# Moving one batch of the shared experts beside the row scatter, and splitting the filling products behind the routed experts

## The chip, the cores and the metric

The kernel runs on one core of one Trainium2 chip. The time is device microseconds (us) for one execution of the whole program, and the number to compare is the median over several executions. The core has five engines that run at the same time and wait for each other by semaphores: TensorE (PE, matrix products; PEld is its weight load), VectorE (DVE), ScalarE (ACT), GpSimd (POOL) and SyncE (SP, which issues DMAs here).

## The reference

Two decoder layers over x of 4 batches x 512 tokens x 128 features. Each layer adds self-attention, cross-attention to 77 context rows, and a mixture of experts, each on a layer-normalised x. The change is in the mixture of layer 0:

```python
logits = flat @ gate_w                                   # 2048 tokens, 16 experts
scores = softmax(logits) + gate_b
_, topi = top_k(scores, 2)
# each expert: its 320 best tokens of those that chose it (capacity)
idx = top_k(where(assigned, w_tok, -inf), capacity)
y = (silu(xs @ w1) * (xs @ w3) @ w2) * w_tok             # routed, on gathered rows xs
out = zeros.at[idxs].add(ys)
shared = mean over 2 shared experts of (silu(flat @ sw1) * (flat @ sw3)) @ sw2
x = x + out + shared                                     # then layer 1: attention of layernorm(x)
```

## The kernel before

The order on each engine is written out by hand; nothing reorders it but the waits. PSUM has eight banks of 128 x 512 floats, called bank[0] to bank[7]. X holds the residual x; a "batch" is 512 tokens, B = 4, QT = 4 tiles of 128 tokens in each.

**Layer 0's experts.** After the router, DVE works out, for each token and each of its two choices, the row of its expert's list (g_row). Then POOL writes the normalised tokens into the lists in DRAM by 32 indirect DMAs (L658, tensor xs_rows, 2 choices x 16 tiles). SP loads the lists back when all have landed (L510). The routed experts then run on PE, ACT, DVE and POOL in four turns of four experts (routed_turn, the last three in a loop), and SP stores the results (ys_rows, L514). When all are stored, POOL gathers the two result rows of each token of batch 0 by eight indirect DMAs (L670, into big_q and big_k; semaphore got[0]); the gathers of the other batches are spread over layer 1's attention.

**The shared experts** need no list, only hT, the transposed normalised tokens, so they fit anywhere. A unit u = 0 to 15 is a quarter of a batch's hidden features (c = u // 4 is the batch): PE forms two 128 x 512 products in shared_up (L1452; each f32 product shows as two passes in the trace), in banks 4 to 7; ACT takes silu of one (L969), DVE multiplies both (shared_hid, L2223). When the four units of a batch are there, shared_down (L1462, 16 products of 128 x 128, 32 passes) forms the batch's output in bank 0 or 7, and DVE adds half of it to X (shared_add, L2228, semaphore sh_x). Before, batches 0 and 1 (units 0 to 7, then down 0 and down 1) run beside the scatter, and batches 2 and 3 behind the routed experts, both in the order of all units first, then both downs.

**Filling products.** keep_busy (L1182) multiplies an identity into an unused bank; the result is never read. There are three in front of the routed experts (they wait for r_pad, which POOL sets by a memset between its last two scatters, L657), four behind the shared experts, and seven before the first scores of the attention.

**The start of layer 1's attention.** DVE's pre_norm(0, ...) adds the gathered rows of batch 0, weighted, to X (add_expert, L2255, four calls that each raise f0_x by one, so f0_x is 4 when the batch is complete), takes statistics (L1824, L1866), a scale by a few tiny steps, and writes ln_h (L2265, semaphore la_h). PE transposes ln_h (L1552), ACT copies it (L1023), and the projections, the spreading of queries and keys by DMA, and then the scores (L1633) follow. DVE's shared_add of the last two batches stands behind ln_h.

Of the kernel before, what the change touches and what calls it, by code (L numbers as in the profile page):

```python
# [14 lines left out]
ALU = mybir.AluOpType  # L15
# [4 lines left out]
P = 128  # L20
B, SEQ, D = 4, 512, 128
# [9 lines left out]
NSH = 2  # L31
# [73 lines left out]
def decoder_kernel(nc, a, out):  # L105
    ctx = ExitStack()
    with ctx:
# [10 lines left out]
        def sem(name):  # L118
            return ctx.enter_context(nc.semaphore(name))

        psum = ctx.enter_context(nc.psum_tensor("psum", [P, 8, 512], F32))
        bank = [psum[:, i, :] for i in range(8)]
# [112 lines left out]
        sh_hidden = [arena[:, 1 + i, :, :] for i in range(2)]  # L235
# [111 lines left out]
        sh_h, sh_silu, sh_hid, sh_y, sh_x, f0_x = (  # L347
            sem(n) for n in ("sh_h", "sh_silu", "sh_hid", "sh_y", "sh_x", "f0_x"))
# [70 lines left out]
        def f1_of(it, p):  # L419

            return {(11, 0): (0, 0), (11, 3): (0, 1), (12, 0): (1, 0), (12, 3): (1, 1), (15, 3): (2, 0), (15, 4): (2, 1)}.get((it, p))

        PRE_NORM = {1: 1, 3: 2, 7: 3}
        ADD_AT = {(1, False): 1, (2, True): 2, (6, True): 3}
        X1_NORM = {b * QT: b - 1 for b in range(1, B)}
        F1_NORM = {(10, False): 0, (11, True): 1, (14, True): 2}
        SCALE_AT = {(it, 5): ("pre", b) for it, b in PRE_NORM.items()}
        SCALE_AT.update({(it, 7): ("x1", b) for it, b in X1_NORM.items()})
        SCALE_AT.update({(9, 7): ("f1", 0), (11, 2): ("f1", 1), (14, 6): ("f1", 2)})

        def scale_count(kind, b):

            return NT + B + [SCALE_AT[at] for at in sorted(SCALE_AT)].index((kind, b))
# [160 lines left out]
        def _(pool):  # L594
# [32 lines left out]
            def batch_norm(b, scales, h):  # L627
                bt = slice(b * QT, (b + 1) * QT)
                pool.wait_ge(ln_mean_ok, scales)
                for _ in range(3):  # L630
                    chained(pool.tensor_tensor(ln_new[:, bt], ln_rstd[:, bt], ln_var[:, bt], ALU.mult))
                    chained(pool.tensor_tensor(ln_new[:, bt], ln_new[:, bt], ln_rstd[:, bt], ALU.mult))
                    chained(pool.tensor_scalar(ln_new[:, bt], ln_new[:, bt], -0.5, 1.5, ALU.mult, ALU.add))
                    chained(pool.tensor_tensor(ln_rstd[:, bt], ln_rstd[:, bt], ln_new[:, bt], ALU.mult))
                chained(pool.tensor_tensor(ln_h[:, bt, :], X[:, bt, :], bcast(ln_mv[:, bt, 0], 2, D), ALU.subtract))
                pool.tensor_tensor(ln_h[:, bt, :], ln_h[:, bt, :], bcast(ln_rstd[:, bt], 2, D), ALU.mult).then_inc(h, 1)
# [107 lines left out]
            def add_experts(b):  # L744
                pool.wait_ge(got[b], 16 * 2 * QT)
                for c in range(2):
                    if c:
                        pool.wait_ge(f0_x, b * 4 + 2)
                    bt = slice(b * QT, (b + 1) * QT)
                    chained(pool.tensor_tensor(gathered[c][:, bt, :], gathered[c][:, bt, :], bcast(g_w[:, c, bt], 2, D), ALU.mult))  # L750
                    pool.tensor_tensor(X[:, bt, :], X[:, bt, :], gathered[c][:, bt, :], ALU.add).then_inc(f0_x, 2)

            def guest_norm(it, late):
                if (it, late) in ADD_AT:
                    add_experts(ADD_AT[it, late])
                if late and it in PRE_NORM:
                    b = PRE_NORM[it]
                    batch_norm(b, scale_count("pre", b), la_h)
# [71 lines left out]
        def _(act):  # L830
# [134 lines left out]
            def shared_silu(u):  # L965
                act.wait_ge(sh_h, u + 1)
                if u >= 2:
                    act.wait_ge(sh_hid, u - 1)
                act.activation(silu[:, u % 2, :], bank[4 + 2 * (u % 2)][:, :], ACT.Silu).then_inc(sh_silu, 1)  # L969
# [11 lines left out]
            def routed_turn(j, first):  # L981
                for k in range(4):
                    routed_silu(j * 4 + k)
                    if k:
                        routed_y(j, k - 1)
                    if k in (0, 2) and not first:
                        act.wait_ge(ys_out[k // 2], j * 16)
                routed_y(j, 3)
# [16 lines left out]
            act.activation(k1T[:, :], bank[4][:, 0:B * LK], ACT.Identity, bias=x1b[:, 1:2]).then_inc(pre_act, 1)  # L1005
            act.wait_ge(pre_mm, 5)
            act.activation(vx1[:, :, :], bank[5][0:LK, :].rearrange("p (b d) -> p b d", b=B), ACT.Copy).then_inc(pre_act, 1)
            for u in range(8):
                shared_silu(u)
            routed_turn(0, True)  # L1010
            with act.Fori(1, E0 // 4) as j:
                routed_turn(j, False)
            for u in range(8, 16):
                shared_silu(u)
            warm(ACT.Exp)

# [158 lines left out]
        def _(pe):  # L1175
            def keep_busy(o, times, small=False):

                for _ in range(times):
                    if small:
                        pe.matmul(o[:, 0:P], ones[:, :], ones[:, :], start=True, stop=True)  # L1180
                    else:
                        pe.matmul(o, ident, cst[:, 0:SEQ], start=True, stop=True)  # L1182
# [154 lines left out]
            for b in range(B):  # L1337
                pe.wait_ge(ln_out, X0 * B + b + 1)
                for i in range(2):
                    mm = pe.matmul(bank[2 * b + i][:, :], x0w[:, i, :], hT[:, b * SEQ:(b + 1) * SEQ], start=True, stop=True)  # L1340
# [76 lines left out]
            for t in range(1, NT + 4):  # L1417
# [5 lines left out]
                u = (t - 3) // 2  # L1423
# [23 lines left out]
            def shared_up(u):  # L1447
                c, e = u // 4, E0 + u // 2 % 2
                if u >= 2:
                    pe.wait_ge(sh_hid, u - 1)  # L1450
                for w in range(2):
                    mm = pe.matmul(bank[4 + 2 * (u % 2) + w][:, :], w13[:, e, w, u % 2 * P:(u % 2 + 1) * P],  # L1452
                                   hT[:, c * SEQ:(c + 1) * SEQ], start=True, stop=True)
                mm.then_inc(sh_h, 1)

            def shared_down(c):
                pe.wait_ge(sh_hid, 4 * c + 4)
                if c >= 2:
                    pe.wait_ge(sh_x, c - 1)
                for t in range(QT):  # L1460
                    for k in range(4):
                        mm = pe.matmul(bank[7 * (c % 2)][:, t * P:(t + 1) * P], sh_hidden[c % 2][:, k, t * P:(t + 1) * P],  # L1462
                                       w2[:, E0 + k // 2, k % 2, :], start=(k == 0), stop=(k == 3))
                mm.then_inc(sh_y, 1)

# [45 lines left out]
            for i in range(2):  # L1511
                mm = pe.transpose(bank[1][:, i * P:(i + 1) * P], g_wm[:, i * NT // 2:(i + 1) * NT // 2, :].rearrange("p t e -> p (t e)"), ident)
# [8 lines left out]
            for i in range(2):  # L1521
                mm = pe.transpose(bank[1][:, i * P:(i + 1) * P], (g_lo, g_hi)[i][:, :].broadcast_to([P, P]), ident)
# [4 lines left out]
            pe.matmul(bank[3][:, :], ones[:, :], kinds, start=True, stop=True).then_inc(g_mm, 1)  # L1527
            pe.matmul(bank[2][:, :], tri, kinds, start=True, stop=True).then_inc(g_mm, 1)

            def shared_chunks(first, last):  # L1530
                for u in range(4 * first, 4 * last):
                    shared_up(u)
                for c in range(first, last):
                    shared_down(c)

            pe.wait_ge(pre_act, 3)
            shared_chunks(0, 2)
            pe.wait_ge(r_pad, 1)
            keep_busy(bank[2], 3)
            routed_turn(0, True)  # L1540
# [1 line left out]
                routed_turn(j, False)  # L1542
            routed_down(E0 - 1, 3, False)
            pe.wait_ge(r_yc, E0)
            shared_chunks(2, 4)
            pe.wait_ge(ld_a1, 112)
            def pre_part(b, part):
                o = pre_bank(b, part)
# [48 lines left out]
            def f1_part(b, part):  # L1597
# [6 lines left out]
                if part == 1:  # L1604
# [2 lines left out]
                        mm = pe.matmul(o[:, t * E1:(t + 1) * E1], hT_b[:, t * P:(t + 1) * P], gw1[:, :], start=True, stop=True)  # L1607
                    mm.then_inc(g_mm, 1)

            keep_busy(bank[1], 4)  # L1610
            for part in range(5):
                pre_part(0, part)
# [196 lines left out]
        def _(dve):  # L1809
# [223 lines left out]
            for t in range(NT + 4):  # L2033
# [4 lines left out]
                u = (t - 4) // 2  # L2038
# [179 lines left out]
            def shared_hid(u):  # L2218
                c = u // 4
                dve.wait_ge(sh_silu, u + 1)  # L2220
                if c >= 2 and u % 4 == 0:
                    dve.wait_ge(sh_y, c - 1)
                dve.tensor_tensor(sh_hidden[c % 2][:, u % 4, :], bank[5 + 2 * (u % 2)][:, :], silu[:, u % 2, :], ALU.mult).then_inc(sh_hid, 1)  # L2223

            def shared_add(c):
                dve.wait_ge(sh_y, c + 1)
                xc = X[:, c * QT:(c + 1) * QT, :]
                dve.scalar_tensor_tensor(xc, bank[7 * (c % 2)][:, :].rearrange("p (t d) -> p t d", d=D), 1.0 / NSH, xc, ALU.mult, ALU.add).then_inc(sh_x, 1)  # L2228

            for u in range(8):  # L2230
                shared_hid(u)
            for c in range(2):
                shared_add(c)
            routed_turn(0, True)
            with dve.Fori(1, E0 // 4) as j:
                routed_turn(j, False)
# [5 lines left out]
            dve.tensor_copy(embpad[:, edge + NPOS:], emb[:, NPOS - 1:NPOS].broadcast_to([HD, 2 * SEQ - 1 - edge - NPOS])).then_inc(a1_emb, 1)  # L2242
            dve.tensor_scalar(a1bs[:, :], a1b[:, 0:1], SCALE1, None, ALU.mult).then_inc(a1_bias, 1)
            dve.tensor_scalar(a1bb[:, 0, :], a1bb[:, 0, :], SCALE1, None, ALU.mult).then_inc(a1_bias, 1)
            for u in range(8, 16):
                shared_hid(u)

            def add_expert(b, c, half):
# [9 lines left out]
            def pre_stats(b, first, last):  # L2258
                dve.wait_ge(f0_x, b * 4 + 4)
                for t in range(b * QT + first, b * QT + last):  # L2260
                    norm_stats(t)
# [20 lines left out]
            def pre_stats_of(it, p):  # L2282

                if it in PRE_NORM and p in (4, 5):
                    pre_stats(PRE_NORM[it], 2 * p - 8, 2 * p - 6)

# [128 lines left out]

            for step in range(12):
                pre_norm(0, step)
            for c in range(2, B):
                shared_add(c)
            dve.wait_ge(sh_x, B)  # L2420
            dve.wait_ge(r_y, E0)
            pre_part(0, 1)
# [246 lines left out]
```

## Time and profile before

| | us |
|---|---|
| median of 3 runs | 1402.18 |
| lowest, highest | 1400.52, 1410.3 |
| the profiled execution, its own time | 1399.95 |
| its span in the profile | 1398.2 |

The profile is of one execution. PE is a matmul's pass, PEld a weight load that overlaps it. "<-" in brackets names what ended an engine's idle time. PEclk is the clock that was granted to TensorE: 1.0 is 2.4 GHz, 0.50 is 1.2 GHz. Times are counted from the span's start. The page's busy shares by fortieths of the span show PE full nearly everywhere, with a dip from about 0.43 to 0.52 of the span:

```profile
PE   8999999999999779860749988989999999989998
```

The dip is the router with its search for each expert's threshold, and then the scatter; the last low slice, the 21st (699 to 734 us), holds the end of the scatter.

### The profile page before, as it was taken

Reading aid. Unit: us, or ns where it says so; the run is one execution under the profiler, and the core shown is the slowest. Engines: PE = TensorE matmul, PEld = TensorE weight load, DVE = VectorE, ACT = ScalarE, POOL = GpSimd, SP = SyncE. Lnnn points to the kernel's source line nnn. Section 1 sums busy time; section 2 is a strip of 40 time slices with the busy share of each in tenths; the row PEclk is TensorE's granted clock in tenths of the full one; section 3 lists DMA queues with packets and bytes.
Section 4 is the critical chain, followed back from the end, with each engine's and each line's share of the span. In section 5 each row is a group of like instructions: output and inputs, shape, how many; then the busy total and the mean of one; then the engine's idle time right before and its main releaser. Section 6 shows DMA issues by size and latency. Waiting matters only on the chain.

```text
span 1398.2 us, 29260 instructions
## 1 busy us (share of the span) xinstructions
PE 1257.2 (90%) x10872; PEld 920.3 (66%) x10872; DVE 969.2 (69%) x2337; ACT 712.8 (51%) x1473; POOL 617.3 (44%) x756
## 2 busy tenths in 40 slices
PE   8999999999999779860749988989999999989998
PEld 5667676777777546540437656767777777767887
DVE  5988877777777678768413466666777888776554
ACT  4566666666666536620103335655666666633222
POOL 3565555555555311120541348685565655402110
PEclk9999999999999979965879999999999999999999
DMA  5131000000000100000013123211120210000001
GB/s 182 48 122 32 1 1 1 1 1 2 1 1 1 52 18 2 2 1 0 6 46 106 50 53 114 59 41 38 39 54 24 47 45 25 8 1 0 1 0 30
DMA packets 77000, 43.88 MB, mean 31 GB/s; under 512 B 26089, under 2 KB 71738, under 8 KB 76870
## 3 DMA queue, kind: packets, MB, share of 16 engines
q1 hardware_dynamic: 72342, 38.56, 10.4%
q10 hardware_dynamic: 2480, 2.29, 0.5%
q8 instruction: 84, 1.38, 0.4%
q0 software_dynamic: 2048, 1.27, 0.4%
q14 instruction: 46, 0.38, 0.1%
HBM read 21.89 MB, written 10.49 MB: 23 GB/s over the span
## 4 chain that ended last, share of the span: by engine, by line
PE 68%; DVE 16%; POOL 5%; ACT 4%; issue 4%; SPq 2%; DMA 1%; ACTq 0%; POOLq 0%; DVEq 0%
PE psum L1270 8%; PE psum L1255 7%; PE psum L1649 7%; PE psum L1245 6%; PE psum L1758 6%; PE psum L1769 4%; PE psum L1661 4%; PE psum L1633 3%; PE psum L1640 3%; PE psum L1481 3%; PE psum L1221 2%; POOL xs_rows L658 2%; PE psum L1279 2%; DVE negmax L2438 2%; SPq L571 2%
## 5 line engine op out<-in xcount | busy, mean ns | idle before, releaser
L606 POOL TENSOR_TENSOR arena<-arena,rden 128x512 f32<-128x512 f32 x256 | 260.6, 1040 | 209.9 <-DVE rden L1920 209.8
L893 ACT ACTIVATE arena<-psum,negmax 128x512 f32<-128x512 f32 x256 | 175.0, 692 | 150.9 <-DVE negmax L1911 131.6
L1911 DVE TENSOR_REDUCE negmax<-psum 128x1 f32<-128x512 f32 x256 | 168.0, 681 | 55.5 <-PE psum L1245 54.9
L2438 DVE TENSOR_REDUCE negmax<-psum 128x1 f32<-128x512 f32 x256 | 164.4, 684 | 53.1 <-PE psum L1640 51.1
L1255 PEld LDWEIGHTS psum<-cst,arena 128*128 128x128 f32 x1024 | 113.1, 141 | 44.7 <-issue 44.3
L1255 PE MATMUL psum<-cst,arena 128*128 128x128 f32 x1024 | 138.1, 276 | 3.1 <-DVE arena L1906 0.8
L1633 PE MATMUL psum<-a_kstack,a_qblk 96*128 96x512 f32 x256 | 96.5, 458 | 13.4 <-DMA a_kstack<-a_klo 8.6
L1245 PE MATMUL psum<-a_qk 64*128 64x512 f32 x768 | 106.0, 407 | 2.5 <-DVE a_qk L1929 2.5
L1758 PE MATMUL psum<-f_h,f_w 128*128 128x512 f32 x384 | 101.3, 414 | 7.0 <-DVE arena L2536 6.9
L1142 ACT ACTIVATE arena<-psum 128x512 f32<-128x512 f32 x64 | 38.1, 597 | 108.3 <-PE psum L1758 108.3
L1245 PEld LDWEIGHTS psum<-a_qk 64*128 64x128 f32 x768 | 67.4, 184 | 38.9 <-issue 24.2
L1099 ACT ACTIVATE kT<-psum,negmax 128x512 f32<-128x512 f32 x64 | 44.0, 687 | 90.6 <-PE psum L1649 74.5
L1758 PEld LDWEIGHTS psum<-f_h,f_w 128*128 128x128 f32 x384 | 72.3, 196 | 24.4 <-issue 7.9
L2442 DVE COPY arena<-psum 128x512 f32<-128x512 f32 x128 | 87.1, 681 | 1.3 <-PE psum L1649 1.2
L720 POOL TENSOR_TENSOR a_qblk<-a_qstack,cst 96x512 fp32r<-96x512 f32 x64 | 68.6, 1072 | 28.4 <-PE psum L1640 23.0
L1093 ACT ACTIVATE arena<-psum 128x512 f32<-128x512 f32 x128 | 76.1, 595 | 1.6 <-PE psum L1649 1.6
L1640 PEld LDWEIGHTS psum<-w,wqkv 128*64 128x64 f32 x1024 | 45.7, 137 | 47.2 <-issue 47.2
L2536 DVE TENSOR_TENSOR arena<-psum,arena 128x512 f32<-128x512 f32 x64 | 44.1, 691 | 42.3 <-ACT arena L1142 42.2
L1099 ACT ACTIVATE hst<-psum,negmax 128x512 f32<-128x512 f32 x64 | 44.0, 688 | 55.6 <-DVE negmax L2438 51.1
L1640 PE MATMUL psum<-w,wqkv 128*64 128x88 f32 (+3 forms) x1024 | 68.5, 254 | 0.0
L723 POOL TENSOR_TENSOR wqkv<-big_k,cst 128x512 f32<-128x512 f32 x64 | 67.5, 1054 | 0.0
L1661 PE MATMUL psum<-arena,w 128*32 128x128 f32 x2048 | 64.2, 279 | 0.7 <-DVE arena L2442 0.7
(350 smaller groups left out, 2718.8 us busy)
## 6 DMA issues: line engine op xcount, KB each, us to landing
w<-in_ew SPq DMA_DIRECT2D x2, 2048.0 KB, 8.2
a_kstack<-a_khi SPq DMA_DIRECT2D x64, 64.0 KB, 2.0
xs_rows<-f SPq DMA_DIRECT2D x3, 1024.0 KB, 5.3
arena<-xs_rows SPq DMA_DIRECT2D x8, 384.0 KB, 3.7
ys_rows<-wqkv SPq DMA_DIRECT2D x8, 384.0 KB, 2.6
a_kstack<-a_klo SPq DMA_DIRECT2D x32, 64.0 KB, 2.0
a_kstack<-a_khi SPq DMA_DIRECT2D x64, 32.0 KB, 1.9
a_qstack<-a_qhi SPq DMA_DIRECT2D x120, 16.0 KB
```

The lines of the kernel that those rows point to most:

```text
L606: pool.tensor_tensor(a0_p[u % 4], a0_p[u % 4], rden[:, u:u + 1].broadcast_to([P, SEQ]), ALU.mult).then_inc(a0_norm, 1)
L893: act.activation(a0_p[u % 4], bank[u % 4][:, :], ACT.Exp, bias=negmax[:, u:u + 1], accum_out=den[:, u:u + 1]).then_inc(a0_exp, 1)
L1245: mm = pe.matmul(bank[2 * (p % 2) + h][:, :], a0_qk[g % 2][r:r + DK, q, p * P:(p + 1) * P], a0_qk[g % 2][r:r + DK, k, :], start=(i == 0), ...
L1255: mm = pe.transpose(bank[4 + u % 2][:, kt * P:(kt + 1) * P], a0_p[u % 4][:, kt * P:(kt + 1) * P], ident)
L1270: mm = pe.matmul(bank[7][h * DK:(h + 1) * DK, qs], a0_vtok[g % 2][:, kt, h * DK:(h + 1) * DK], a0_pT[g % 2][h][:, kt, qs], start=(kt == 0) ...
L1633: pe.matmul(bank[n % 4][:, :], qblk[:, hg, j, lg:lg + 2, :, :].rearrange("p g h l -> p (g h l)"), kstack[it % 2][:, n // 4, :], start=True ...
L1640: mm = pe.matmul(bank[n % 4][blk * HQ * LG:(blk + 1) * HQ * LG, t * P + low:t * P + high], rblk[:, hg, j, g, :, :].rearrange("p h l -> p ( ...
L1649: mm = pe.transpose(bank[4 + n % 2][:, kt * P:(kt + 1) * P], ptile[n % 4][:, kt * P:(kt + 1) * P], ident)
L1661: mm = pe.matmul(bank[6][32 * j:32 * j + 32, grp * P:(grp + 1) * P], vst[:, kt, hg * HG + grp * 4 + j, :], a1_pT(hg, kt, grp, j), start=(k ...
L1758: mm = pe.matmul(bank[2 * (u % 2) + w][:, :], w_parts[:, e, wp, w * FF + hf * P:w * FF + (hf + 1) * P], h_parts[hp][:, c * SEQ:(c + 1) * S ...
L1911: dve.tensor_reduce(negmax[:, u:u + 1], bank[u % 4][:, :], AX.X, ALU.max, negate=True).then_inc(a0_max, 1)
L2438: dve.tensor_reduce(negmax[:, n % 8:n % 8 + 1], bank[n % 4][:, :], AX.X, ALU.max, negate=True).then_inc(a1_max, 1)
```

## The change

Batch 2 of the shared experts (units 8 to 11 and its down product) moves from behind the routed experts to beside the scatter, on PE, ACT and DVE. Its order there is: units 0 to 7, down 0, units 8 to 11, down 1, down 2. Down 1 now writes bank 1 instead of 7 (since units 8 to 11 use bank 7), and down 2 still bank 0, down 3 bank 7. Behind the routed experts stay units 12 to 15, down 3 and one shared_add. The filling products there grow from four to seven: three at once, then a wait until f0_x is 4, then four.

```diff
+        SHARED_BANK = (0, 1, 0, 7)
...
-            for u in range(8):
+            for u in range(12):
                 shared_silu(u)
             routed_turn(0, True)
             with act.Fori(1, E0 // 4) as j:
                 routed_turn(j, False)
-            for u in range(8, 16):
+            for u in range(12, 16):
                 shared_silu(u)
...
             pe.wait_ge(pre_act, 3)
-            shared_chunks(0, 2)
+            for u in range(8):
+                shared_up(u)
+            shared_down(0)
+            for u in range(8, 12):
+                shared_up(u)
+            shared_down(1)
+            shared_down(2)
             pe.wait_ge(r_pad, 1)
             keep_busy(bank[2], 3)
...
             pe.wait_ge(r_yc, E0)
-            shared_chunks(2, 4)
+            for u in range(12, 16):
+                shared_up(u)
+            shared_down(3)
             pe.wait_ge(ld_a1, 112)
...
+            keep_busy(bank[1], 3)
+            pe.wait_ge(f0_x, 4)
             keep_busy(bank[1], 4)
             for part in range(5):
                 pre_part(0, part)
...
             for u in range(8):
                 shared_hid(u)
-            for c in range(2):
-                shared_add(c)
+            shared_add(0)
+            for u in range(8, 12):
+                shared_hid(u)
+            shared_add(1)
+            shared_add(2)
             routed_turn(0, True)
...
-            for c in range(2, B):
-                shared_add(c)
+            shared_add(3)
```

PE beside the scatter, before: 16 up products of two batches, 32 down products, three fillers, and the first routed expert's transposes.

```order
L1528 MATMUL psum<-arena,cst 128x512
L1452 MATMUL psum<-hT,w 128x512 x16
L1462 MATMUL psum<-w,arena 128x128 x32
L1182 MATMUL psum<-cst 128x512 x3
L1471 MATMUL psum<-cst,arena 128x128 x6
L1481 MATMUL psum<-wqkv,arena 128x320 x8
```

The same place after (lines are one further down):

```order
L1529 MATMUL psum<-arena,cst 128x512
L1453 MATMUL psum<-hT,w 128x512 x16
L1463 MATMUL psum<-w,arena 128x128 x16
L1453 MATMUL psum<-hT,w 128x512 x8
L1463 MATMUL psum<-w,arena 128x128 x32
L1183 MATMUL psum<-cst 128x512 x3
```

Eight up products and one batch's down products are new, between down 0 and the fillers.

PE behind the routed experts, before, from the last unit on, with the semaphores that a product waits for:

```order
L1452 MATMUL psum<-hT,w 128x512 [waits sh_hid]
L1452 MATMUL psum<-hT,w 128x512
L1462 MATMUL psum<-w,arena 128x128 [waits sh_x,sh_hid]
L1462 MATMUL psum<-w,arena 128x128 x15
L1462 MATMUL psum<-w,arena 128x128 [waits sh_x,sh_hid]
L1462 MATMUL psum<-w,arena 128x128 x15
L1182 MATMUL psum<-cst 128x512 [waits ld_a1]
L1182 MATMUL psum<-cst 128x512 x3
L1552 MATMUL psum<-cst,ln_h 128x128 [waits la_h]
L1552 MATMUL psum<-cst,ln_h 128x128 x3
```

And after:

```order
L1453 MATMUL psum<-hT,w 128x512 [waits sh_hid]
L1453 MATMUL psum<-hT,w 128x512
L1463 MATMUL psum<-w,arena 128x128 [waits sh_x,sh_hid]
L1463 MATMUL psum<-w,arena 128x128 x15
L1183 MATMUL psum<-cst 128x512 [waits ld_a1]
L1183 MATMUL psum<-cst 128x512 x2
L1183 MATMUL psum<-cst 128x512 [waits f0_x]
L1183 MATMUL psum<-cst 128x512 x3
L1555 MATMUL psum<-cst,ln_h 128x128 [waits la_h]
L1555 MATMUL psum<-cst,ln_h 128x128 x3
```

One down batch is gone, so the only down left stands right behind the last unit, and the fillers are in two groups with a wait for f0_x between them.

## Rows read from the trace of the kernel before

**Rows 1.** The page: busy time, share of the span and instructions of each engine.
```profile
PE 1257.2 (90%) x10872; PEld 920.3 (66%) x10872; DVE 969.2 (69%) x2337; ACT 712.8 (51%) x1473; POOL 617.3 (44%) x756
```

**Rows 2.** Timeline, POOL: start us, duration, engine, line, operation, [idle before <- releaser].
```profile
675.97 1.31 POOL L658 DMA_INDIRECT xs_rows<-ln_h,g_row  x1 [56.72 <-DVE g_m L2213]
...
689.07 0.97 POOL L658 DMA_INDIRECT xs_rows<-ln_h,g_row  x1 [0.30 <-issue]
...
712.04 0.97 POOL L658 DMA_INDIRECT xs_rows<-ln_h,g_row  x1 [0.30 <-issue]
```

**Rows 3.** Timeline, PE, beside the scatter.
```profile
690.22 7.31 PE L1462 MATMUL psum<-w,arena 128*128 128x128 f32 x64
715.94 4.99 PE L1182 MATMUL psum<-cst 128*128 128x512 f32 x6 [18.42 <-POOL wqkv L657]
```

**Rows 4.** The chain that ended last: start us, us, what; end of the scatter.
```profile
716.05 2.16 DMA xs_rows<-ln_h,g_row
...
721.84 0.56 PE psum L1471 x3
```

**Rows 5.** Timeline, PE, behind the routed experts.
```profile
786.44 14.00 PE L1452 MATMUL psum<-hT,w 128*128 128x512 f32 x32 [0.58 <-ACT wqkv L978]
800.28 7.31 PE L1462 MATMUL psum<-w,arena 128*128 128x128 f32 x64
807.42 3.60 PE L1182 MATMUL psum<-cst 128*128 128x512 f32 x8
810.86 0.60 PE L1552 MATMUL psum<-cst,ln_h 128*128 128x128 f32 x4
```

**Rows 6.** Timeline, POOL: first and last of eight gathers; then their line's landing times.
```profile
789.97 1.08 POOL L670 DMA_INDIRECT big_q<-ys_rows,g_row  x1 [13.88 <-DMA ys_rows<-wqkv]
...
799.16 1.00 POOL L670 DMA_INDIRECT big_k<-ys_rows,g_row  x1 [0.30 <-issue]
...
DMA to landing us min/median/max: 2.5/2.6/6.9
```

**Rows 7.** Timeline, DVE, in both places.
```profile
689.33 0.69 DVE L2223 TENSOR_TENSOR arena<-psum,arena 128x512 f32<-128x512 f32 x1 [1.02 <-ACT arena L969]
...
794.24 0.69 DVE L2223 TENSOR_TENSOR arena<-psum,arena 128x512 f32<-128x512 f32 x1 [1.02 <-issue]
...
801.84 1.14 DVE L2255 SCALAR_TENSOR_TENSOR X<-big_q,g_w,X 128x128 f32<-128x128 f32 x4
...
807.89 1.12 DVE L2265 TENSOR_SCALAR ln_h<-X,ln_mv,ln_rstd 128x128 f32<-128x128 f32 x4
808.92 1.28 DVE L2228 SCALAR_TENSOR_TENSOR X<-psum,X 128x512 f32<-128x512 f32 x2
```

**Rows 8.** The chain that ended last, start of layer 1's attention.
```profile
811.54 0.61 ACT w L1023
...
823.76 0.71 PE psum L1633 x2
```

**Rows 9.** Stretches: from:to us, length, busy us (instructions) by engine, PEclk, DMA share, GB/s.
```profile
697.60:699.60 2.00, 0.00 (x0) 0.00 (x0) 0.65 (x1) 0.00 (x0) 1.39 (x3) 1.00 0.08 26
700.00:715.80 15.80, 0.00 (x0) 0.00 (x0) 0.00 (x0) 0.00 (x0) 12.15 (x14) 0.50 0.08 22
...
822.00:823.60 1.60, 0.00 (x0) 0.00 (x0) 0.00 (x0) 0.00 (x0) 1.60 (x2) 1.00 0.54 130
...
826.20:828.80 2.60, 0.00 (x0) 0.00 (x0) 1.04 (x2) 2.06 (x4) 2.05 (x3) 0.50 0.27 64
829.00:832.80 3.80, 3.80 (x19) 3.00 (x20) 1.98 (x3) 0.72 (x2) 3.80 (x4) 0.50 0.11 26
...
863.10:865.70 2.60, 0.00 (x0) 0.00 (x0) 2.33 (x6) 1.22 (x3) 2.60 (x4) 1.00 0.19 51
865.90:867.00 1.10, 1.10 (x12) 0.74 (x14) 1.00 (x9) 0.35 (x1) 1.10 (x2) 1.00 0.52 148
867.10:870.00 2.90, 2.90 (x60) 2.90 (x58) 2.33 (x5) 1.77 (x3) 2.36 (x7) 0.50 1.04 349
```

More of the change, by code:

```diff
@@ L1461, in shared_down @@
                     for k in range(4):
-                        mm = pe.matmul(bank[7 * (c % 2)][:, t * P:(t + 1) * P], sh_hidden[c % 2][:, k, t * P:(t + 1) * P],
+                        mm = pe.matmul(bank[SHARED_BANK[c]][:, t * P:(t + 1) * P], sh_hidden[c % 2][:, k, t * P:(t + 1) * P],
                                        w2[:, E0 + k // 2, k % 2, :], start=(k == 0), stop=(k == 3))
@@ L1528, in _ @@
             pe.matmul(bank[2][:, :], tri, kinds, start=True, stop=True).then_inc(g_mm, 1)
[L1530 to L1534, printed above, removed]
-            pe.wait_ge(pre_act, 3)
-            shared_chunks(0, 2)
+            pe.wait_ge(pre_act, 3)
+            for u in range(8):
[5 more added lines that the diff above has]
+            shared_down(2)
             pe.wait_ge(r_pad, 1)
@@ L2227, in shared_add @@
                 xc = X[:, c * QT:(c + 1) * QT, :]
-                dve.scalar_tensor_tensor(xc, bank[7 * (c % 2)][:, :].rearrange("p (t d) -> p t d", d=D), 1.0 / NSH, xc, ALU.mult, ALU.add).then_inc(sh_x, 1)
+                dve.scalar_tensor_tensor(xc, bank[SHARED_BANK[c]][:, :].rearrange("p (t d) -> p t d", d=D), 1.0 / NSH, xc, ALU.mult, ALU.add).then_inc(sh_x, 1)
             for u in range(8):
                 shared_hid(u)
-            for c in range(2):
-                shared_add(c)
+            shared_add(0)
[3 more added lines that the diff above has]
+            shared_add(2)
             routed_turn(0, True)
@@ L2244, in _ @@
             dve.tensor_scalar(a1bb[:, 0, :], a1bb[:, 0, :], SCALE1, None, ALU.mult).then_inc(a1_bias, 1)
-            for u in range(8, 16):
+            for u in range(12, 16):
                 shared_hid(u)
```

## The prediction

> **What bounds the kernel now.** I read the page first: TensorE (PE) is busy 90% of the span, VectorE (DVE) 69%, so only places where PE waits, or does work that others wait for, can move the end [rows 1]. The change touches two such places. I read their timelines engine by engine, then the waits, then the clock by stretches.
>
> Place one is the scatter of token rows. GpSimd (POOL) issues 32 indirect DMAs, one per 1.27 us (0.97 and 0.30 before it), from 675.97 on, the last at 716.05 [rows 2, 4]. PE does the shared experts of batches 0 and 1 beside it: its last up products run to 690.3, its down products from 690.22 to 697.5, and then it idles 18.42 us for POOL's pad memset [rows 3]. The expert rows come by DMA behind the last scatter, and the first routed transpose starts at 721.84 [rows 4]. So POOL bounds this place, with 18 us of PE room.
>
> Place two lies behind the routed experts. PE turns from them at 786.44; then it does 32 up passes (14.00 us), 64 down passes (7.31), 8 filling passes (3.60), and at 810.86 the transposes of the layer-1 attention's first batch [rows 5]. Beside that, POOL issues eight gathers from 789.97, the last at 799.16, landing 2.5 to 2.6 us after issue, so at 801.7 [rows 6]. DVE starts adding gathered rows at 801.84, straight behind its last shared product and with no wait, and has ln_h, which the transposes read, at 807.89 + 1.12 = 809.0 [rows 7]. PE takes it only at 810.86: ln_h lies ready for 1.86 us while PE ends work that the next stage doesn't need. That is what the change can win at once. All behind it hangs on these transposes: the copy at 811.54, and in the end the first scores at 823.76 [rows 8].
>
> **The change, part by part.**
> *Batch 2 goes to the scatter.* It adds 16 up passes and 32 down passes there. From rows at full clock: 14.00 / 32 x 16 = 7.0 us and 7.31 / 2 = 3.65 us [rows 5]. The new order is up 0 to 7, down 0, up 8 to 11, down 1, down 2. Up 8 waits for product 6, long done, and DVE's product 8 for down 0, which precedes it in PE's order; ScalarE and DVE keep up with a unit (0.69 us of product after 1.02 us of idle [rows 7]), so nothing new waits. PE ends near 697.5 + 10.6 = 708.1, 7.8 us before it is let go at 715.94. DVE adds 4 x 0.69 + 0.69 us. Sum at this place: 0. If that cover were gone, each us beyond 7.8 would delay the routed experts by one.
> *PE's clock there.* It was 1.0 until 699.6 and 0.50 from 700 to 715.8 [rows 9], and the six filling passes behind that took 4.99 us [rows 3], where eight at full clock take 3.60 [rows 5]. With 7.8 us of idle instead of 18.4 I expect the same: the fall came within 2.5 us. Cost 0; if the clock stays up, these six end about 2.3 us earlier, which nobody waits for.
> *Batch 3 alone goes behind the routed experts.* PE starts it at 786.44 as before. Four units take 7.0 us, to 793.3. Now there is a wait that was not there: down 3 needs the product of unit 15, which was hidden behind down 2. The fourth product of before shows when that is: 794.24 + 0.69 = 794.93 [rows 7]. So down 3 runs 795.0 to 798.6, and the first three fillers (6 passes, 6 x 0.43 = 2.6) to 801.2.
> *The wait for f0_x.* Behind it on PE's queue are four fillers and then the transposes, for which ScalarE and all of the next stage wait. DVE is free since 794.93, so its adds wait for the gathers: the start moves from 801.84 to about 801.75, a gain of 0.1 and no more, since POOL's chain (store landed, eight issues) isn't touched. The eight adds take 2 x 1.14 us [rows 7] and end at 804.1. PE idles 801.2 to 804.1, 2.9 us. Four fillers take 3.6 us [rows 5], to 807.7. ln_h is ready at 808.9 to 809.0, so DVE is late next, and PE starts the transposes there: 810.86 - 809.0 = 1.9 us sooner.
> *The clock in this place.* Before, PE was busy without a break and granted 1.0. Now it idles 1.7, 2.9 and 1.3 us. Idle 822.0 to 823.6 kept 1.0, but idle 826.2 to 828.8 was at 0.50, and so were the 3.8 us of work from 829.0 to 832.8; and after idle 863.1 to 865.7 PE worked 1.1 us at full clock and fell to 0.50 at 867.1 [rows 9]. 2.9 us is nearest to the last two (2.6 each), so I expect a fall in most executions. Its price: a filler pass takes 0.85 us at the low level (six took 4.99 us at 715.94, the last of them quicker [rows 3]) against 0.43. As in the row of 829, low for 3.8 us after the restart: 804.1 + 3.8 = 807.9 with 4.5 passes done, the other 3.5 to 809.5. Gain then 1.3 instead of 1.9. Bounds: no fall, 1.9; all eight low, 6.8 us, 810.9, and the four transposes (0.60 us [rows 5]) at half rate too: 0 to 0.6 us worse than before. I take 1.6, the middle of the two likely ones. A page of the Trainium skill, "TensorE: Matmul & The Clock Gate" (section "Why this matters for your kernels"), asks for no idle gaps above about 3 us; by it the clock would hold and the gain be 1.9, but the trace shows falls around gaps of 2.6 us, and I go by the trace.
> *The rest.* The layer-1 pipeline is only started sooner; DVE's batch-3 sum after ln_h is now one of 0.69 us instead of two (1.28), off the path. Bank changes (0, 1, 0, 7) put no new reader before a writer that waits.
>
> **Sum.** 0 + 0 - 0.1 - 1.5 = -1.6 us. On the profiled execution, 1399.95, that is 1398.3; it lies 2.2 us below the median of the runs shown, 1402.18, and the prediction for the median is 1400.6.
>
> **Rivals.**
> *1. The clock eats it (15%).* Low through all eight fillers and the transposes. For it: the rows at 826 and 867. Against: PE would have to be low for 7 us of unbroken work, while the low stretch at 829 ended after 3.8 us of work. Result -0.1 to +0.6: 1402.1 to 1402.8.
> *2. The scatter gets slower (5%), the other sign.* If POOL's issues had to wait for DVE's added work, four products and a sum of 0.69 us, the routed experts start up to 3.5 us later, and the time is 1402.2 + 3.5 - 1.6 = 1404.1; it decides from 1.6 us of added delay. Against it: the issue at 689.07 took 0.97 us after 0.30 while DVE ran a product at 689.33, and the one at 712.04, with DVE idle, the same 0.97 after 0.30 [rows 2, 7]. The Trainium skill, "SBUF — State Buffer" (section "SBUF: two separate sides"), says that some DVE operations lock GpSimd out of a shared port, so that it can't write descriptors. By that rule, were these operations of that kind, this rival would hold; the spacing above speaks against it for these very operations.
> *3. More than the sum (12%).* The next stage starts elsewhere in the clock's course, and the low stretch 829.0 to 832.8 [rows 9] goes away: 3.8 us at half rate, 1.9 us back. 1400.6 - 1.9 = 1398.7. Nothing in the change causes it.
> *4. No effect (8%).* The 12 us from the transposes' copy to the first scores [rows 8] hold DMAs and work of all engines, and one of them is held by something that doesn't move, say the copies of the position table by SP's queue. For it: that DMA queue isn't in my rows. Against: each piece of that chain follows the one before it. Result: 1402.2.
>
> **How the numbers follow.** The forecast, DVE's ln_h chain as the new bound and a gain of 1 to 2 us, has 60%: 1400.6. The four runs of before spread from 1399.95 to 1410.3, far more than the gain; that spread sets the range more than the cases do. Below: rival 3's 1398.7 less 1.7 (median less lowest run) is 1397. Above: rival 2's 1404.1 and a little spread, 1405. A change of 1% is 14 us, and about what a measurement of this kernel can tell from none; no case comes near it, also not 18 us of PE room at the scatter, which was idle time off the path. Faster 3%, same 94%, slower 3%, the small ones for mechanisms that I don't see.
>
> **What would show it.** In the profile after: PE's down products of the scatter end near 708 and its idle before the fillers is near 8 us; the first routed transpose still near 721.8; down 3 near 795.0; two idles of PE, some 1.7 and 2.9 us; the transposes at 809.0 to 809.5, now waiting for DVE's ln_h; the first scores 1.3 to 1.9 us sooner than 823.76. Wrong would be: scatters spaced wider than 1.27 us, transposes that start right behind the fillers after 810.4, or a stage behind that takes a different time by more than 2 us.

## The result, and the profile after

The changed kernel took 1413.8 us (median of four, 1411.89 to 1423.17) against 1401.67 of the kernel before (four, 1400.52 to 1410.3): a ratio of 1.0077, 95% interval 1.0045 to 1.0109. The interval lies wholly above 1, so this is a slowdown, small but clear of the noise: under the 1% of which the prediction spoke, and 8.8 us above its range. The profiled execution took 1414.77 us, its span is 1412.8 (before 1399.95 and 1398.2).

The page, engine totals and PE's busy tenths:

```profile
PE 1257.0 (89%) x10878; PEld 918.0 (65%) x10878; DVE 969.5 (69%) x2337; ACT 712.3 (50%) x1473; POOL 618.3 (44%) x756
...
PE   8999999999999779842649978989999999989998
```

The work is that of [rows 1]; the time is idle time. The row of tenths hardly shows where: its 18th to 20th slices read 4, 2, 6 for 6, 0, 7 before, the 24th 7 for 8, and each slice is 0.4 us longer now, so that they cover other stretches. The timeline shows it. PE's timeline beside the scatter (start, duration, idle before and what ended it), which answers [rows 3]:

```profile
691.55 3.73 PE L1463 MATMUL psum<-w,arena 128*128 128x128 f32 x32
695.12 3.60 PE L1453 MATMUL psum<-hT,w 128*128 128x512 f32 x8
724.46 5.55 PE L1453 MATMUL psum<-hT,w 128*128 128x512 f32 x8 [25.74 <-DVE arena L2228]
729.84 7.31 PE L1463 MATMUL psum<-w,arena 128*128 128x128 f32 x64
736.98 2.74 PE L1183 MATMUL psum<-cst 128*128 128x512 f32 x6
739.56 0.82 PE L1472 MATMUL psum<-cst,arena 128*128 128x128 f32 x6
```

PE does down 0 and units 8 and 9, then stands 25.74 us in front of unit 10, which needs the product of unit 8. The first routed transpose comes at 739.56 instead of 721.84 [rows 4]. DVE's timeline shows that DVE is not the late one:

```profile
692.38 0.69 DVE L2228 TENSOR_TENSOR arena<-psum,arena 128x512 f32<-128x512 f32 x1 [1.02 <-ACT arena L970]
723.02 0.69 DVE L2233 SCALAR_TENSOR_TENSOR X<-psum,X 128x512 f32<-128x512 f32 x1 [29.95 <-remote]
723.71 1.29 DVE L2228 TENSOR_TENSOR arena<-psum,arena 128x512 f32<-128x512 f32 x2
```

It waits 29.95 us to add down 0, whose last pass ended on PE at 695.3. ACT, which takes the first product of units 8 and 9, is as late:

```profile
723.08 1.08 ACT L970 ACTIVATE arena<-psum 128x512 f32<-128x512 f32 x2 [30.73 <-remote]
```

The profile finds no instruction that released it ("remote"), and the chain of the end says the same:

```profile
691.77 31.29 another core or an unknown queue
```

So what PE had finished was not known to DVE or ACT for some 28 us. (The ends of PE's passes are modelled in the profile, so it can't tell a result that was late from a report that was late; "report" stands for both below.) Meanwhile POOL kept its pace of 0.97 us after 0.30 to its last scatter at 717.70, and SP, which waits for the scatters to land, was told in time: its load of the lists starts 2.2 us behind the last scatter, while PE's reports are still held. In the undisturbed reload below it is 2.2 us too (716.24 and 718.42).

```profile
719.88 0.96 SPq L511 DMA_DIRECT2D arena<-xs_rows  x2
```

Behind the routed experts, PE's timeline answers [rows 5] and [rows 8]:

```profile
804.11 7.13 PE L1453 MATMUL psum<-hT,w 128*128 128x512 f32 x16 [0.58 <-ACT wqkv L979]
812.65 3.84 PE L1463 MATMUL psum<-w,arena 128*128 128x128 f32 x32 [1.41 <-issue]
816.33 2.74 PE L1183 MATMUL psum<-cst 128*128 128x512 f32 x6
821.66 3.70 PE L1183 MATMUL psum<-cst 128*128 128x512 f32 x8 [2.59 <-DVE X L2263]
826.52 0.66 PE L1555 MATMUL psum<-cst,ln_h 128*128 128x128 f32 x4 [1.16 <-DVE ln_h L2273]
...
839.39 0.70 PE L1638 MATMUL psum<-a_kstack,a_qblk 96*128 96x512 f32 x2 [1.70 <-POOL wqkv L724]
```

The account: the first routed transpose is 17.7 us late (1.6 of it because the first scatter came at 677.53 and not 675.97, a difference of the stage ahead, before anything that was changed; 16.1 beside the scatter). From there to the units behind the routed experts nothing changed, 64.55 us against 64.60. From those units to the first scores it takes 35.28 us against 37.32: 2.0 us won. The scores are 15.6 us late, the span 14.6.

### The profile page after: what moved, and what is told of

It is laid out like the page before. It is cut to its first block, busy times and chain, and to the rows that moved or that the text cites. A ratio compares the mean times of both kernels' runs of the same rounds, so it can differ in the third digit from the quotient of the medians.

```text
span 1412.8 us, 29272 instructions
## 1 busy us (share of the span) xinstructions
PE 1257.0 (89%) x10878; PEld 918.0 (65%) x10878; DVE 969.5 (69%) x2337; ACT 712.3 (50%) x1473; POOL 618.3 (44%) x756
## 3 DMA queue, kind: packets, MB, share of 16 engines
q0 software_dynamic: 2048, 1.27, 0.4%
## 4 chain that ended last, share of the span: by engine, by line
PE 68%; DVE 16%; ACT 4%; issue 3%; POOL 3%; another core or an unknown queue 2%; DMA 1%; SPq 1%; ACTq 0%; DVEq 0%; POOLq 0%
PE psum L1271 8%; PE psum L1256 7%; PE psum L1654 7%; PE psum L1763 6%; PE psum L1246 6%; PE psum L1774 4%; PE psum L1666 4%; PE psum L1638 3%; PE psum L1645 3%; PE psum L1482 3%; PE psum L1222 2%; PE psum L1280 2%; PE psum L1228 2%; PE psum L1234 2%
## 5 line engine op out<-in xcount | busy, mean ns | idle before, releaser
L1143 ACT ACTIVATE arena<-psum 128x512 f32<-128x512 f32 x64 | 38.1, 597 | 108.5 <-PE psum L1763 108.5
L1094 ACT ACTIVATE arena<-psum 128x512 f32<-128x512 f32 x128 | 76.1, 595 | 1.6 <-PE psum L1654 1.6
L970 ACT ACTIVATE arena<-psum 128x512 f32<-128x512 f32 x16 | 9.4, 597 | 110.0 <-PE psum L1453 75.9
```

## The experiments

Theories of the standstill, numbered as the expectations have them. A: PE waits for its own instructions. B: something of the scatter holds PE's reports to the other engines. C: the interleaved order (down 0, then units of batch 2) makes it. D: it belongs to a load or a chip, not to the changed program. E: it belongs to where in the program's instructions this place lies. The experiments ran in four sets, each on a chip of its own (chips 0, 6, 4 and 1 of the record); the kernels of one set share the runs of the kernel before. On which chip the two kernels of the comparison above ran is not recorded.

### First set: one part alone, padding, order, half the scatter

The batch moved, but the filling products left as before (one group of four, no wait for f0_x):

```diff
-            keep_busy(bank[1], 3)
-            pe.wait_ge(f0_x, 4)
             keep_busy(bank[1], 4)
```

> The changed kernel with the four fillers of before and no wait for f0_x, so only batch 2 moves. If the 12 us come from the batch beside the scatter, where TensorE stands still from 698.7 to 724.46 us in the changed kernel's profile, they stay: 1413 to 1415 us, with the same idle of some 25 us. If they came from the split fillers, the time goes back to 1399 to 1402.

Filling products added far ahead, which shifts the later instructions and changes nothing at the scatter:

```diff
                 pe.matmul(bank[2][:, 0:CUTS], ...).then_inc(b_total, 1)
+                keep_busy(bank[3], 3, small=True)
```

> The changed kernel with three small filling products (128x128) behind each of the 16 bisection products, in TensorE's idle time there; they only shift the position of everything behind them in TensorE's instruction stream, by 48 products. The queue that brings TensorE's instructions (q8) shows a packet when TensorE is between units 9 and 10 of the shared experts. Theory A, the stall is tied to that fetch: the packet now comes during the bisection, the stall goes away and the time is 1399 to 1402. Theory B, TensorE's completions are held by the scatter and its end, wherever the fetch lies: the stall stays and the time is 1413 to 1415. If the fillers cost by themselves, that is at most 1 us.

Both downs of batches 0 and 1 ahead of batch 2 (DVE's sum of batch 1 moved likewise):

```diff
             shared_down(0)
+            shared_down(1)
             for u in range(8, 12):
                 shared_up(u)
-            shared_down(1)
             shared_down(2)
```

> The changed kernel with down 1 and its sum ahead of units 8 to 11, as in the kernel before, so that batch 2 comes last on all three engines. Theory A (fetch): TensorE's stop lies at the same count of instructions, 16 products further in the new order's down 1 or in the first of units 8 to 11, and the stall stays in some form. Theory B (scatter holds completions from about 695 on): the sums of DVE at 694 and 698 are missing too. Theory C, the order down 0, units, down 1 is what stalls: the stall is gone, 1399 to 1402 us.

17 scatters instead of 32 (the rows of half of the assignments are not written, SP waits for fewer):

```diff
-                for t in range(NT):
+                for t in range(0 if c == 0 else NT - 1, NT):
...
-            sp.wait_ge(scattered, 16 * 2 * NT)
+            sp.wait_ge(scattered, 16 * (NT + 1))
```

> The changed kernel with 17 of the 32 scatters; the rows of the second choice of all tiles but the last are left out of the experts' lists, so the output isn't the reference's. The scatter ends some 19 us earlier, near 700. Theory A (fetch alone): TensorE's stall keeps its length of some 25 us and ends near 724. Theory B (held until the scatter is done and the first rows come back): it ends some 19 us earlier, near 704, and the whole kernel is some 19 us shorter than the changed one.

Measured, against 1399.28 of before: the batch alone 1400.66 (ratio 1.0009, 0.9987 to 1.0032); padded 1397.73 (0.9988, 0.9967 to 1.0009); downs first 1395.86 (0.9968, 0.9946 to 0.9990); half the scatter 1380.08 (one run). None of the four has the standstill, not even the batch alone, whose instructions at the scatter are those of the changed kernel. That left D, or E with the changed kernel's own layout. The interval of downs first lies below 1, but its profiled execution took 1404.24, so its trace doesn't show where a gain would come from.

The batch alone also says what the split fillers are for. PE's timeline behind the routed experts:

```profile
796.36 3.84 PE L1463 MATMUL psum<-w,arena 128*128 128x128 f32 x32 [1.41 <-DVE arena L2226]
800.04 3.60 PE L1183 MATMUL psum<-cst 128*128 128x512 f32 x8
810.11 1.11 PE L1555 MATMUL psum<-cst,ln_h 128*128 128x128 f32 x4 [6.47 <-DVE ln_h L2271]
811.96 2.08 PE L1560 MATMUL psum<-a1w,w 128*128 128x128 f32 x8 [0.73 <-ACT w L1024]
```

With one group of fillers PE idles 6.47 us, the transposes take 1.11 us instead of 0.60 [rows 5], and the projections 2.08 instead of the 1.16 that they take in the reload below. From the units of batch 3 to the first scores it is 37.23 us, so nothing is left of the gain.

### Second set: the changed kernel again, and the fillers alone

The changed kernel, unaltered:

> The changed kernel, unaltered, loaded anew. Without the split fillers (e1) and with the order of down 1 turned (e3) the stall of 25 us is absent, and up to it e1 is the same program. Theory D, the stall belongs to a load or a chip and not to the program: here it is absent too, TensorE's down 2 ends near 708, the routed transposes start near 722, and the time is 1.5 to 3 us below the kernel before, 1396 to 1399 where that has 1399. Theory E, it belongs to this very program, by where its instructions lie in memory: it is back, and the time is 11 to 14 us above the kernel before.

The kernel before, with the new fillers and their wait only:

```diff
+            keep_busy(bank[1], 3)
+            pe.wait_ge(f0_x, 4)
             keep_busy(bank[1], 4)
```

> The kernel before, with the seven fillers of the change in place of four (three, the wait for f0_x, four), and batches 2 and 3 both behind the routed experts as before. TensorE ends down 3 at 807.4, when f0_x has long been 4, so the seven fillers run in one piece to 813.4 instead of 811.0: by the trace 2.6 us slower than before, 1401 to 1402 where before has 1399. If the fillers were free, no difference.

The changed kernel took 1396.6 us against 1399.75 (ratio 0.9988, 0.9966 to 1.0010). PE's timeline, both places:

```profile
692.80 7.03 PE L1453 MATMUL psum<-hT,w 128*128 128x512 f32 x16
699.67 7.31 PE L1463 MATMUL psum<-w,arena 128*128 128x128 f32 x64
716.13 4.33 PE L1183 MATMUL psum<-cst 128*128 128x512 f32 x6 [9.15 <-POOL wqkv L658]
721.79 0.88 PE L1472 MATMUL psum<-cst,arena 128*128 128x128 f32 x6 [1.34 <-DMA arena<-xs_rows]
...
786.39 7.13 PE L1453 MATMUL psum<-hT,w 128*128 128x512 f32 x16 [0.58 <-ACT wqkv L979]
794.94 3.84 PE L1463 MATMUL psum<-w,arena 128*128 128x128 f32 x32 [1.41 <-DVE arena L2228]
798.61 2.74 PE L1183 MATMUL psum<-cst 128*128 128x512 f32 x6
803.98 5.40 PE L1183 MATMUL psum<-cst 128*128 128x512 f32 x8 [2.63 <-DVE X L2263]
809.22 0.60 PE L1555 MATMUL psum<-cst,ln_h 128*128 128x128 f32 x4
...
822.03 0.71 PE L1638 MATMUL psum<-a_kstack,a_qblk 96*128 96x512 f32 x2 [1.70 <-POOL wqkv L724]
```

The same program, and no standstill: the downs end at 707.0, the routed experts start at 721.79. So program order and placement alone (A, C, E) don't decide it. The fillers alone took 1402.47 (1.0022, 1.0007 to 1.0037), and the scores are 40.04 us behind the first unit where before it was 37.32: three more fillers on a path that has no room for them cost 2.7 us. Each half of the change alone is thus no gain; only together do they win at the tail.

### Third set: a third load, and the two best edits together

> The changed kernel a third time, unaltered, loaded anew. Theory D (the standstill of 25.7 us in front of expert hidden unit 10 belongs to a load or a chip and not to the program): if this load has it, TensorE idles over 20 us between the up products of batch 2, the first routed transpose comes after 735 us and the ratio is above 1.005; if not, the PE rows of the scatter stage are those of the reload before it (16 up products of batch 2's pair in one run of 7.0 us behind down 0, fillers near 716, first routed transpose near 721.8) and the ratio is 0.998 to 0.999. Theory A to C (something in the program does it): the standstill is back here.

> The changed kernel with both of the edits that were tried apart: three small filling products behind each of the 16 bisection products, and down 1 with its sum ahead of batch 2's hidden units. If the two gains are of different places they add: the profile shows the first routed transpose near 721.8, the fillers of the second piece at 3.70 us (full clock) and not 5.40, first scores near 821.5, and the ratio is near 0.9955. If the gains measured for them apart were scatter between loads, the ratio is that of the changed kernel reloaded, 0.998 to 0.999.

The changed kernel took 1415.29 us against 1407.11 (ratio 1.0068, 1.0039 to 1.0097), and the two edits together 1418.0 (1.0091, 1.0063 to 1.0119). The hold of PE's reports is back in both. PE's timeline of the changed kernel:

```profile
693.94 3.60 PE L1453 MATMUL psum<-hT,w 128*128 128x512 f32 x8
723.07 5.68 PE L1453 MATMUL psum<-hT,w 128*128 128x512 f32 x8 [25.53 <-DVE arena L2228]
```

With both edits it looks otherwise. Down 1 follows down 0 there with its inputs ready, so PE doesn't stand; from 693 to 720 its passes go one at a time, and the first routed transpose is no earlier (738.25, against 738.31 in the changed kernel):

```profile
718.96 0.37 PE L1463 MATMUL psum<-w,arena 128*128 128x128 f32 x1 [1.73 <-issue]
720.36 1.87 PE L1463 MATMUL psum<-w,arena 128*128 128x128 f32 x8 [1.03 <-issue]
```

This is a different chip from the first two sets, and here the kernel before is slower too, 1407.11 where it had 1399.3 and 1399.8. Whether the two edits add could therefore not be seen. The DMA view from 692 to 722 us of this run and of the reload speaks against A. In the undisturbed reload PE's instruction queue moves one packet in this stretch:

```profile
q8 instruction: 1, 0.02, 0.3%
```

In the run with the standstill no such row is there: PE, which stood, asked for no instructions, and none was on its way. Its packet comes only behind 722, when PE goes on. In the trace after it comes at 726, so the packet which the expectation of the padded run puts between units 9 and 10 lies behind the standstill and not in it. The page "Runtime: NRT & Kernel Launch" of the Trainium skill (section "Instruction fetch mechanics") says that fetching a block is mostly hidden; by it A would cost next to nothing, and the trace agrees.

### Fourth set: the kernel before on such a chip

The kernel before, the half scatter again, and the changed kernel as the marker, one run each, on a chip that none of the sets above had:

> The kernel before, unaltered, profiled anew beside the changed kernel. The standstill has now been seen on two chips and was absent on two others. If it is a state of the chip in which TensorE's reports to the other engines are held from some 17 us behind the first scatter until the first expert rows land, the kernel before has it too on such a chip, where nothing on TensorE waits for a report: down 1 ends near 697.5, VectorE's sum of it, which starts at 697.6 on an undisturbed chip, comes only near 720 to 722, and the expert part starts at about its old time (first routed transpose 722 to 724). If the hold belongs to the changed program, the sum stays at 697.6. On an undisturbed chip this profile repeats the one of before within 1 us.

> The changed kernel with 17 of the 32 scatters (the output lacks the rows of half of the assignments), again, for a chip that has the standstill. Scatter stage ends some 19 us sooner, last scatter near 697 to 699. If the hold is tied to the scatters' rows on their way, TensorE's units 8 to 11 run in one run of 7.0 us or with a pause of under 5 us in which the hold ends with the scatters (near 700), and the first routed transpose is near 708. If it is tied to a position in the program or to a fixed time, the pause is still over 15 us. On an undisturbed chip: no pause, transpose near 708, 1380 us.

> The changed kernel unaltered, as the marker of the chip: with the standstill it idles over 20 us in front of expert hidden unit 10 and takes 1410 to 1420 us; without it, batch 2's units run in one run of 7.0 us and it takes 1393 to 1402 us.

They took 1405.35, 1392.77 and 1410.05 us (the kernel before beside them 1403.47), and the marker has the standstill (25.95 us in front of unit 10, first routed transpose at 737.52). So the kernel before can be read on such a chip. PE's timeline:

```profile
688.95 4.74 PE L1462 MATMUL psum<-w,arena 128*128 128x128 f32 x41
...
698.85 0.37 PE L1462 MATMUL psum<-w,arena 128*128 128x128 f32 x1 [1.16 <-issue]
...
719.90 0.37 PE L1462 MATMUL psum<-w,arena 128*128 128x128 f32 x1 [1.73 <-issue]
721.31 1.87 PE L1462 MATMUL psum<-w,arena 128*128 128x128 f32 x8 [1.04 <-issue]
722.97 4.07 PE L1182 MATMUL psum<-cst 128*128 128x512 f32 x6
726.88 0.82 PE L1471 MATMUL psum<-cst,arena 128*128 128x128 f32 x6
```

and DVE's, and the waits from 675 to 745 us:

```profile
721.38 0.69 DVE L2228 SCALAR_TENSOR_TENSOR X<-psum,X 128x512 f32<-128x512 f32 x1 [30.91 <-remote]
...
PE psum L1462 <- issue: 22.6, 15, 2.4
```

The kernel before has the hold as well. Its sum of down 0, at 693.99 in the undisturbed trace, comes at 721.38. More than that: from 694 on, the passes of down 1 go singly, one each 1.4 to 2.8 us, waiting for nothing in the program (22.6 us in 15 waits for "issue"), where an undisturbed trace has all 64 down passes in 7.31 us [rows 3]. But only the last eight passes of down 1 and the fillers are left when it ends, and most of the hold lies in what were 18.42 idle us [rows 3]: the first routed transpose is at 726.88, 5.0 us later than in [rows 4] (the expectation had 722 to 724). The changed kernel on the same chip has it at 737.52, so the change costs 10.6 us at this place.

What the hold hangs on, the half scatter shows. Its PE, DVE and POOL timelines:

```profile
694.06 3.60 PE L1453 MATMUL psum<-hT,w 128*128 128x512 f32 x8
702.22 6.03 PE L1453 MATMUL psum<-hT,w 128*128 128x512 f32 x8 [4.57 <-DVE arena L2228]
```

```profile
700.79 0.69 DVE L2233 SCALAR_TENSOR_TENSOR X<-psum,X 128x512 f32<-128x512 f32 x1 [8.78 <-remote]
```

```profile
697.14 0.97 POOL L659 DMA_INDIRECT xs_rows<-ln_h,g_row  x1 [0.17 <-issue]
```

The last scatter is issued at 697.14 instead of near 716, and the hold ends at 700.79 instead of 721.4 (3.7 us behind the last scatter, against 5.4 in the kernel before, issued at 715.95). It starts alike in both: 13 to 18 us behind the first scatter (675.86 and 676.20). In the half scatter DVE still takes its product at 691.32 at the usual pace, and down 0, done at 694.1, is not seen. PE's pause is 4.57 us, as expected of a hold that is tied to the scatters. But the first routed transpose comes at 717.81 and not near 708, since 17.0 us of work lie behind the end of the hold here too. B is shown in this part, by one run of each kernel: on such a chip, PE's reports are held while the scatters run, and set free shortly behind the last. Not shown is what stands in their way, and why some chips have it. That it goes by the chip rests on the sets: five of five kernels have it on two chips, none of six on the other two.

One sign points to the records of the profiler. In the runs with the hold the DMA view has no landing time for the scatter, in those without it has; the kernel before on the last chip, and the reload, from 676 to 722 us:

```profile
xs_rows<-ln_h,g_row POOLq DMA_INDIRECT x32
```

```profile
xs_rows<-ln_h,g_row POOLq DMA_INDIRECT x32, 2.1
```

But the sign is weaker than it looks. From 676 to 690 us, while DVE still gets every product on time, the landing time is missing already in the runs with the hold. And in the undisturbed trace of the kernel before, the gathers behind the routed experts have none either (from 786 to 815 us), though nothing stands still there:

```profile
big_q<-ys_rows,g_row POOLq DMA_INDIRECT x4
```

So the runs with the hold lose records, but a place that loses records needn't have the hold. What speaks for the records is that the passes which crept one by one in the kernel before signal no one; what each of them does leave is a record. The Trainium skill, "NOTIFIC — Programmer's Manual" (section "The design, and what it trades"), says that a full record queue can be set to overwrite, to drop, or to stall whoever writes into it. A stall of PE would look like the creeping passes, and dropped records like the missing landing times; no run here shows which setting holds, or that either causes the hold. Every timed execution lists a span and a clock and so was recorded too; whether an unrecorded one has the hold is open.

## Why the prediction was right and wrong

**Batch 2 goes to the scatter, "nothing new waits", "Sum at this place: 0".** This is the step that failed, for the executions compared. The sum of engine times was right: undisturbed, the downs end at 707.0 (forecast 708.1), PE idles 9.15 us (7.8), the first transpose is at 721.79 (721.8). But units 10 and 11 wait for DVE and ACT, and so for reports of PE, in a stretch in which the kernel before has nothing on the path that waits for one (only DVE's two sums do). With the hold, 15.1 us of work, from unit 10 to the fillers, lies behind its end (724.46 to 739.56) instead of under it, so that the term put at 0 measured 17.7 us between the two traces, and 10.6 on one chip. The prediction itself had the price, "each us beyond 7.8 would delay the routed experts by one", but took the cover for safe because PE was idle there. Idle time of PE isn't the same as time in which PE and DVE can hand work to each other.

**The profile of before could not show it.** In [rows 9] DVE has its sum of down 1 between 697.6 and 699.6, so that trace is from an execution without the hold, and the trace after from one with it. Comparing the two puts 17.7 us at the first routed transpose on the change (16.1 without the later first scatter); on one and the same chip it is 10.6 (737.52 against 726.88).

**The clock at the scatter.** Forecast 4.99 us again for the six filling passes, or 2.3 less; undisturbed they took 4.33 to 5.05 us, hidden.

**Behind the routed experts.** Forecast against the reload: down 3 at 795.0, 794.94; PE's idles 1.7 and 2.9, 1.41 and 2.63; DVE's adds from 801.75 to 804.1, 801.61 to 803.93; transposes at 809.0 to 809.5, 809.22; scores 1.3 to 1.9 us sooner, 35.64 us behind the first unit against 37.32, 1.7. All steps held, so the forecast's mechanism was right on an undisturbed chip, for this place and for the scatter. With the trace after it was 2.0 us.

**The clock there.** I expected a fall in most executions; three of seven had one. The four filler products behind the idle took 3.70 us, full clock, after idles of 2.59, 2.62, 2.56 (the changed kernel in the comparison, the third and the fourth load) and 2.58 (padded), and 5.40 after 2.63, 2.72 and 2.66 (reload, downs first, both edits). The granted clock of the reload, stretches ahead of and in the fillers:

```profile
801.30:803.90 2.60, 0.05 (x1) 0.00 (x0) 2.25 (x8) 0.00 (x0) 0.74 (x2) 1.00 0.00 0
804.00:809.20 5.20, 5.20 (x8) 2.15 (x9) 4.72 (x25) 0.00 (x0) 0.00 (x0) 0.67 0.00 0
```

The Trainium skill, "TensorE: Matmul & The Clock Gate" (section "Why this matters for your kernels"), asks for no gaps above about 3 us; the traces agree in four executions and not in three, where the clock fell behind gaps of 2.63 to 2.72 us. It cost 0.4 us (scores 35.64 us behind the first unit against 35.28 in the trace after), where the forecast had 0.6.

**Rivals.** Rival 2, a slower scatter, had the right sign and place and the wrong mechanism: POOL's spacing never changed. Rivals 1, 3 and 4 didn't occur. That the tail's gain reaches the end is likely and not proved: 0.9988 on an undisturbed chip is -1.7 us, and its interval holds 1. Where the hold is, routed transposes 10.6 us later, less 1.8 at the tail (scores 35.38 us behind the first unit in the marker, 37.22 in the kernel before beside it), make 8.8; the third load measured 8.2. That these agree is partly luck: on the fourth chip the scores are 8.8 us apart, but the two times only 4.7 (1410.05 and 1405.35), and the reload won 1.7 us at the scores but has a span 5.4 us shorter than before. What comes behind the scores varies by some us from execution to execution, as much as the gain at the tail.

**The range.** 1397 to 1405 was made from the spread of one chip's runs. The kernel before alone has medians of 1399.3 to 1407.1 over the chips here, and the undisturbed reload, 1396.6, lies just below the range too.

## What to carry to other kernels

Before you fill an engine's idle time, ask not only whether the engine is free but whether the new work needs a hand-over there, and whether the old work did: a stretch in which nothing on the path waited says nothing about how long a wait takes in it. Work with its inputs ready was no safe cover here either: with the hold, the passes of down 1 crept. What counted was how much was left to do when the hold ended: 5.6 us in the kernel before (721.31 to 726.88), 15.1 in the changed one, 17.9 with both edits (720.36 to 738.25). And take a second load on another chip before you put a standstill of tens of us on a line of the program: here one kernel, unaltered, measured 0.1% faster on one and 0.7% slower on another.

## What the hardware did that was not expected

On two of the four chips, and in the profiled execution of the comparison, TensorE's finished work was not seen by the other engines for 27 to 29 us: from 13 to 18 us behind the first of 32 indirect scatters until 5.2 to 5.4 us behind the last, with the scatters issued at an unchanged 1.27 us. Completions of the scatters themselves reached SP in time. With 17 scatters it was 6.7 us (down 0 done at 694.1, taken at 700.79, 3.7 us behind the last). It hides in the kernel before at a price of 5.0 us. Nothing in the program differs between a load of the changed kernel with it and one without. That kernel's times fall apart in the same way: 1410.05 to 1423.8 us in the three loads whose trace has the hold, 1392.73 to 1404.75 in the one whose trace has not.
